# Layer 3 of a four-layer graph network makes its messages by rows of 128 edges into a ring

## The chip, the cores and the metric

The kernel runs on one core of one Trainium2 chip. The metric is device time in microseconds (us) of one execution. The engines are TensorE (PE, with its weight loads as PEld), VectorE (DVE), ScalarE (ACT), GpSimd (POOL) and SyncE (SP, which here only issues DMAs and waits).

## The reference

Four residual layers on 6250 nodes with 128 features and 100,000 edges, sorted by their target node. Each layer normalizes, applies relu, passes messages along the edges and adds the result. Layer 3 is the one that changes:

```python
s = s @ (w_lin1_s / sqrt(32));  v = einsum('nui,uw->nwi', v, w_lin1_v / sqrt(32))   # per node
h = silu(edge_scalars @ (fc_w1 / sqrt(8))) * SILU_NORM       # 8 -> 64, per edge
w0, w1, w2, w3 = split(h @ (fc_w2 / sqrt(64)), 4)            # 64 -> 4 x 32
se, ve = s[edge_src], v[edge_src];  es, ev = edge_attr[:, :1], edge_attr[:, 1:4]
mid_s0 = w0 * se * es;              mid_s1 = w3 * einsum('eui,ei->eu', ve, ev) / SQRT3
mid_v0 = (w1 * se)[:, :, None] * ev[:, None, :];   mid_v1 = (w2 * es)[:, :, None] * ve
ns, nv = segment_sum(mid_scal, edge_dst) / 4, segment_sum(mid_vec, edge_dst) / 4
x = x + concat(ns @ w_lin2_s, nv @ w_lin2_v)
```

A message has 256 numbers per edge.

## The kernel before, in words

The edges stand in DRAM as 782 rows of 128. Nodes are in 50 blocks of 128. As edges are sorted by target, a row belongs to one block or to a few that follow each other. The setup makes a list of items, one for each pair of a row and a block that it touches: 832 places in all (`ITEMS`), 208 groups of four (`QUADS`). A row that touches two blocks stands in two items. Tables per item lie in SBUF: source nodes `src_it`, target within the block `rel_it`, and as registers' food the block (`blk_row`) and the row (`row_row`).

Layer 3's edge loop works by quads of items. In step q, in the order of each engine's own list:

- SP (`load_small_rows`, lines 449 to 465) waits for DVE and ACT to be done with quad q-8 (two calls of `held`, each a wait and a semaphore increment, lines 240 to 243) and loads for each of the four items its row of `e_a8` (L463) and of `e_a4` (L464). Every fourth quad it loads 16 registers with row numbers (L455).
- POOL (L670) gathers table rows by source node into `G`, a ring of 16 items, four DMAs per quad; it waits for the products of the quad four before.
- PE: first layer of the MLP of quad q-1 (L871), transpose of the attributes of quad q (L878), aggregation of quad q-4 by a one-hot matrix (L887), second layer of the MLP of quad q-2 (L897).
- ACT: copies the transpose (L1075), applies silu (L1080), scales messages (L1087, L1091).
- DVE (`edges3`, lines 1517 to 1574): adds the four aggregates of quad q-5 to the accumulator of their blocks (helper at L1388), with a register load of block numbers every fourth quad (L1524), products of quad q-3 (L1545, L1551, L1563, L1567, L1569, L1572), one-hot of quad q-1 (L1375).

The messages lie in `msg3`, a ring of four quads, and are read at the place where they were written. `quad_steps` (L268) writes the loop: 8 steps ahead, a hardware loop of 8 steps per turn, the rest behind. No planner is at work; the order is the written one, and each engine waits on semaphores that count the others' steps. Before the loop, SP loads the MLP's weights (`load_fc`, L467) and stores the node tables (`store_table`, L370). After it, `node_updates` multiplies by `w_lin2` and adds to `X`, 13 batches of up to four blocks, and SP stores each.

Layers 1 and 2 have loops of the same kind, and gather at L670 too.

Of the kernel before, what the change touches and what calls it, by code (L numbers as in the profile page):

```python
# [25 lines left out]
P = 128  # L26
N = 6250
E = 100000
D = 128
# [22 lines left out]
QUADS = ITEMS // 4  # L52
NODE_BATCH = (4, 4, 2, 4)
# [4 lines left out]
def gnn_layers(nc, x, src, dst, edge_attr_4, edge_attr_64, edge_attr_8, edge_weight,  # L58
               W0, gamma, beta, Wmsg, bmsg, Wupd, bupd, w1, b1, w2, b2, wg, bg, wu, bu,
               wl1s, wl1v, fc1, fc2, wl2s, wl2v, out):  # L60
    with ExitStack() as ctx:
# [8 lines left out]
        def dram(name, shape, dt=F32):  # L70
# [4 lines left out]
        e_a4, e_a8, e_a64 = dram("e_a4", [2 * EPAD, 4]), dram("e_a8", [2 * EPAD, 8]), dram("e_a64", [2 * EPAD, 64])  # L75
        e_pre = dram("e_pre", [QUADS + 4, P, 4, 256])
# [6 lines left out]
        X = sb("X", [P, NBT, D])  # L83
        big = sb("big", [P, BIGW])
# [4 lines left out]
               big[:, 0:NBT * L3W].rearrange("p (b f) -> p b f", f=L3W)]  # L89
# [51 lines left out]
        spare3 = big[:, NBT * L3W:BIGW]  # L141
        fc1q = spare3[0:32, 0:256].rearrange("p (a b) -> p a b", b=P)
        fc2q = spare3[:, 256:512]
        pr3 = spare3[:, 512:2560].rearrange("p (s j c t f) -> p s j c t f", s=2, j=4, c=2, t=4)
        msg3 = spare3[:, 2560:6656].rearrange("p (s j f) -> p s j f", s=4, j=4)
        tmp3 = spare3[:, 6656:6912].rearrange("p (j t f) -> p j t f", j=4, t=2)
        sum3 = spare3[:, 6912:7040].rearrange("p (j f) -> p j f", j=4)
# [44 lines left out]
        inputs_in, weights_in, const_ready, x_in = sem("inputs_in"), sem("weights_in"), sem("const_ready"), sem("x_in")  # L192
# [90 lines left out]

        def landed(each, ring, q, k, lag):
# [62 lines left out]
        def _(sp):  # L347
# [5 lines left out]
            sp.wait_ge(x_in, 1)  # L353
# [95 lines left out]
            def load_small_rows():  # L449

                ph = EDGE[3]
                regs = [sp.alloc_register(f"arow_{k}") for k in range(RING)]

                def top(item):
                    sp.load(regs, row_row[0:1, bass.ds(item + LEAD, RING)])  # L455

                def body(q, k, live):
                    if live(8):
# [1237 lines left out]
```

## Time and profile before

| what | value |
|---|---|
| median of 3 runs (lowest, highest) | 6580.35 us (6579.94, 6586.99) |
| profiled execution, own time | 6581.73 us |
| its span (first to last instruction) | 6580.1 us |
| mean granted TensorE clock | 0.718 of 2.4 GHz |
| busy: PE, DVE, ACT, POOL | 4451.8, 3511.6, 1918.0, 3778.7 us |
| gathers at L670 (three layers) | 2496, 2417.5 us busy, mean 969 ns |

How to read the rows further down. A row of busy time by stretch has the window, its length, then the busy us (and count) of PE, PEld, DVE, ACT and POOL, the granted clock of PE, the mean busy share of the DMA engines and GB/s. A row of waits has the total us, how often, and the longest. A row of a group has count, busy us and mean ns, then the engine's idle time before it and what ended most of it. A row in order of time has start, duration, engine, line and operation; "SPq" is SP's queue, and a bracket tells the idle time before. In the chain, "issue" is time in which the engine waited for nothing that the profile shows.

### The profile page before, as it was taken

Reading aid. Unit: us, or ns where it says so; the run is one execution under the profiler, and the core shown is the slowest. Engines: PE = TensorE matmul, PEld = TensorE weight load, DVE = VectorE, ACT = ScalarE, POOL = GpSimd, SP = SyncE. Lnnn points to the kernel's source line nnn. Section 1 sums busy time; section 2 is a strip of 40 time slices with the busy share of each in tenths; the row PEclk is TensorE's granted clock in tenths of the full one; section 3 lists DMA queues with packets and bytes.
Section 4 is the critical chain, followed back from the end, with each engine's and each line's share of the span. In section 5 each row is a group of like instructions: output and inputs, shape, how many; then the busy total and the mean of one; then the engine's idle time right before and its main releaser. Section 6 shows DMA issues by size and latency. Waiting matters only on the chain. (4 is left out here: it accounts for less than half of the span.)

```text
span 6580.1 us, 113728 instructions
## 1 busy us (share of the span) xinstructions
PE 4451.8 (68%) x21582; PEld 3403.9 (52%) x21583; DVE 3511.6 (53%) x11197; ACT 1918.0 (29%) x5540; POOL 3778.7 (57%) x3395
## 2 busy tenths in 40 slices
PE   1888888888345555656777777777765666666667
PEld 1666666666234444444565656565554444444445
DVE  5655555555443232332655655555565555656555
ACT  2322222222122222222322222222243333333333
POOL 2888888888356666665255555555515454555443
PEclk9555555555577777777889888888886667777667
DMA  4666665666434454444244444444412222222222
GB/s 135 101 90 93 89 93 92 90 92 90 95 112 152 155 156 152 154 154 148 97 138 139 140 136 138 136 141 134 137 55 39 37 38 37 37 38 37 37 38 44
DMA packets 822279, 660.17 MB, mean 100 GB/s; under 512 B 444329, under 2 KB 711251, under 8 KB 820826
## 3 DMA queue, kind: packets, MB, share of 16 engines
q0 software_dynamic: 214432, 287.62, 22.0%
q1 hardware_dynamic: 607674, 370.53, 20.3%
q10 hardware_dynamic: 96, 1.20, 0.1%
q8 instruction: 24, 0.39, 0.0%
q14 instruction: 53, 0.43, 0.0%
HBM read 464.78 MB, written 225.68 MB: 105 GB/s over the span
## 5 line engine op out<-in xcount | busy, mean ns | idle before, releaser
L670 POOL DMA_INDIRECT G<-table,src_it x2496 | 2417.5, 969 | 2121.0 <-issue 651.1
L1388 DVE TENSOR_TENSOR big<-psum,big 128x129 f32 (+2 forms) x2496 | 823.6, 330 | 1225.0 <-remote 596.0
L642 POOL DMA_INDIRECT sums<-work,idx x832 | 1284.1, 1543 | 318.4 <-issue 179.2
L800 PE MATMUL psum<-work 128*128 128x128 f32 x1664 | 631.0, 482 | 192.8 <-DVE work L1435 115.0
L887 PE MATMUL psum<-big,oh 128*128 128x256 f32 x1664 | 643.7, 554 | 8.2 <-ACT big L1091 3.5
L1037 ACT ACTIVATE work<-psum,work 128x128 f32<-128x128 f32 x832 | 305.4, 367 | 1066.4 <-PE psum L792 667.4
L800 PEld LDWEIGHTS psum<-work 128*128 128x128 f32 x1664 | 414.0, 308 | 384.0 <-DVE work L1435 243.5
L747 PE MATMUL psum<-We,work 64*128 64x256 f32 x1664 | 347.0, 552 | 375.1 <-ACT work L1016 295.0
L1375 DVE TENSOR_TENSOR oh<-iota,rel_it 128x512 f32<-128x512 f32 x625 | 438.5, 702 | 298.5 <-remote 143.5
L792 PE MATMUL psum<-big,work 128*128 x1664 | 586.1, 455 | 0.0
L887 PEld LDWEIGHTS psum<-big,oh 128*128 128x128 f32 x1664 | 444.7, 280 | 134.0 <-issue 41.8
L1427 DVE TENSOR_SCALAR work<-G,src_it 128x128 f32<-128x128 int32 x832 | 268.3, 322 | 392.1 <-PE psum L800 308.6
L878 PE MATMUL psum<-ident,work 128*32 128x128 f32 x208 | 69.0, 332 | 557.3 <-DMA work<-e_a 431.6
L747 PEld LDWEIGHTS psum<-We,work 64*128 64x128 f32 x1664 | 212.9, 268 | 435.8 <-issue 352.5
L792 PEld LDWEIGHTS psum<-big,work 128*128 128x128 f32 x1664 | 414.2, 309 | 26.3 <-issue 8.7
L784 PE MATMUL psum<-ident,oh 128*128 128x128 f32 x832 | 366.3, 440 | 83.8 <-issue 46.9
L1050 ACT ACTIVATE work<-psum 128x512 f32<-128x512 f32 x208 | 124.2, 597 | 969.4 <-remote 512.2
L820 PE MATMUL psum<-big,work 128*128 x2496 | 377.0, 300 | 31.2 <-ACT work L1063 28.0
L1009 ACT ACTIVATE work<-psum 128x256 f32<-128x256 f32 x208 | 79.7, 383 | 970.0 <-remote 480.6
L1075 ACT ACTIVATE work<-psum 32x128 f32<-32x128 f32 x208 | 55.4, 266 | 1019.5 <-PE psum L878 676.4
L1493 DVE TENSOR_TENSOR work<-psum,work 128x512 f32<-128x512 f32 x416 | 267.2, 684 | 157.8 <-remote 72.9
L1435 DVE COPY work<-psum 128x128 f32<-128x128 f32 x832 | 242.5, 291 | 179.8 <-DMA sums<-work,idx 172.5
(230 smaller groups left out, 7709.9 us busy)
## 6 DMA issues: line engine op xcount, KB each, us to landing
e_pre<-work SPq DMA_DIRECT2D x208, 512.0 KB
work<-e_pre SPq DMA_DIRECT2D x208, 512.0 KB
G<-e_src SPq DMA_DIRECT2D x832, 64.0 KB
G<-table,src_it POOLq DMA_INDIRECT x2496
work<-e_a SPq DMA_DIRECT2D x832, 32.0 KB
e_a<-in_edge_attr_dram SPq DMA_DIRECT2D x51, 488.0 KB
sums<-work,idx POOLq DMA_INDIRECT x832
work<-e_a SPq DMA_DIRECT2D x832, 4.0 KB
```

Of the source, the lines that this page charges most:

```text
L642: pool.indirect_dma_start(sums[k % COPIES], bass.IndirectOffsetOnAxis(ap=idx[:, k:k + 1], axis=0), z_out[:, k, :], None, compute_op=ALU.ad ...
L670: pool.indirect_dma_start(G[:, k, 0:wid], None, tab, bass.IndirectOffsetOnAxis(ap=src_it[:, n:n + 1], axis=0)).then_inc(quad_in[k // 4], 16)
L747: mm = t.matmul(bank[5 + j % 2][:, j // 2 * 256:j // 2 * 256 + 256], eT1[h:h + 64, (k - 1) % 2, j // 2, :], We2[h:h + 64, :], start=True, ...
L784: t.transpose(bank[s % 2][:, 0:P], oh[:, s, :], ident[:]).then_inc(ph["t_done"], 1)
L792: t.matmul(bank[2 + s % 2][:, 0:P], ohT[:, s % 4, :], at(Tz, b), start=True, stop=True).then_inc(ph["row_done"], 1)
L800: t.matmul(bank[4 + s % 2][:, 0:P], same[:, s % 4, :], scaled[:, s % 4, :], start=True, stop=True).then_inc(ph["sum_done"], 1)
L820: mm = t.matmul(bank[1 + j // 2][:, j % 2 * 256:j % 2 * 256 + 256], ohT2[:, j, :], Qp[:, bass.ds(b, 1), piece * 256:(piece + 1) * 256].rea ...
L887: mm = t.matmul(bank[4 + k % 2 * 2 + j // 2][:, j % 2 * 256:j % 2 * 256 + 256], oh[:, k % 4 * 4 + j, :], msg3[:, k % 4, j, :], start=True, ...
L1037: a.activation(scaled[:, s % 4, :], bank[2 + s % 2][:, 0:P], ACT.Copy, scale=w_it[:, bass.ds(n - 4, 1)]).then_inc(ph["w_done"], 1)
L1375: v.tensor_tensor(oh[:, k % 4 * 4:k % 4 * 4 + 4, :], iota[:].unsqueeze(1).broadcast_to([P, 4, P]), rel_it[:, bass.ds(q * 4, 4)].unsqueeze( ...
L1388: v.tensor_tensor(to, ps, to, ALU.add).then_inc(EDGE[layer]["acc_done"], 1)
L1427: v.tensor_scalar(same[:, s % 4, :], src_b[:, s, :], src_it[:, bass.ds(n - 1, 1)], None, ALU.is_equal).then_inc(ph["same_ready"], 1)
```

## The change

Layer 3 separates what depends only on an edge from what depends on an item. Gather, MLP and products go by rows in their own order: 782 rows, 196 quads (`ROWS4`; the last holds 2). Their messages go to a ring of 64 rows (`RING3`). One-hot, aggregation and adds still go by 832 items; PE reads, for each item, its row from `row_row` and takes the ring's slot row % 64.

- SP loads four rows of an attribute with one DMA, two DMAs per quad, without registers of row numbers.
- POOL gathers with `src_row`, source nodes by row, 782 times. The setup makes this table: two more DMAs on POOL, seven more transposes and copies. It waits in DRAM (`row_cols`) until layer 3.
- PE loads 16 registers every fourth quad (`top`) and reads `msg3` at a slot worked out from them.
- The ring takes 16,384 floats per partition. So `X` and `big` become one tensor, the accumulator of layer 3 moves to the end, and blocks 22 to 49 of `X` (`KEEP` = 22) go to DRAM (`x_keep`) before layer 3's tables are stored and come back after the loop. `pr3`, `tmp3`, `sum3` and the MLP's weights move into `work`.
- `row_steps` writes 16 steps ahead, a hardware loop of 16 steps per turn, and the rest; it tells steps that are live for rows from steps live for items.

```diff
+ROWS4 = (ROWS + 3) // 4
+LAST4 = ROWS - 4 * (ROWS4 - 1)
+RING3 = 64
+KEEP = (NBT * (D + L3W) - RING3 * L3W) // D
...
-        X = sb("X", [P, NBT, D])
-        big = sb("big", [P, BIGW])
+        x_and_big = sb("x_and_big", [P, NBT * D + BIGW])
+        X = x_and_big[:, 0:NBT * D].rearrange("p (b f) -> p b f", f=D)
+        big = x_and_big[:, NBT * D:NBT * D + BIGW]
...
-        msg3 = spare3[:, 2560:6656].rearrange("p (s j f) -> p s j f", s=4, j=4)
+        msg3 = x_and_big[:, KEEP * D:NBT * (D + L3W)].rearrange("p (r f) -> p r f", f=L3W)
+        src_row = view(6144, [META]).bitcast(I32)
...
+        def row_steps(eng, depth, top, body):
+            for q in range(16):
+                if q % 4 == 0:
+                    top(4 * q)
+                body(q, q, lambda lag: q >= lag, lambda lag: q >= lag)
+            whole = ROWS4 // 16 * 16
+            with eng.Fori(16, whole, 16) as q:
+                for k in range(16):
+                    if k % 4 == 0:
+                        top(q * 4 + 4 * k)
+                    body(q + k, k, lambda lag: True, lambda lag: True)
+            for q in range(whole, depth):
+                if q % 4 == 0:
+                    top(4 * q)
+                body(q, q % 16, lambda lag: q - lag < ROWS4, lambda lag: q - lag < QUADS)
...
             def load_small_rows():
-                    for j in range(4):
-                        r = sp.snap(regs[k % 4 * 4 + j], min_val=0, max_val=ROWS - 1)
-                        sp.dma_start(a8q[:, k, j, :], e_a8[bass.ds(r * P, P), :]).then_inc(attr3[k], 16)
-                        sp.dma_start(a4q[:, k, j, :], e_a4[bass.ds(r * P, P), :]).then_inc(attr3[k], 16)
-                quad_steps(sp, 0, top, body, 8)
+                    n = LAST4 if isinstance(q, int) and q == ROWS4 - 1 else 4
+                    at_rows = slice(q * 4 * P, q * 4 * P + n * P) if isinstance(q, int) else bass.ds(q * (4 * P), 4 * P)
+                    for to, of in ((a8q, e_a8), (a4q, e_a4)):
+                        sp.dma_start(to[:, k % 8, 0:n, :], of[at_rows, :].rearrange("(j p) f -> p j f", p=P)).then_inc(attr3[k % 8], 16)
+                row_steps(sp, ROWS4, lambda item: None, body)
...
                 if layer == 3:
                     load_fc()
+                    sp.dma_start(x_keep, X[:, KEEP:NBT, :]).then_inc(kept, 16)
+                    sp.dma_start(src_row, row_cols).then_inc(kept, 16)
+                    sp.wait_ge(kept, 48)
                 if layer:
                     store_table(layer)
                 else:
+                    sp.dma_start(row_cols, m_row).then_inc(kept, 16)
+                    sp.wait_ge(kept, 16)
...
                 barrier(sp)
                 if layer == 3:
+                    sp.dma_start(X[:, KEEP:NBT, :], x_keep).then_inc(kept, 16)
...
-                for n in range(ITEMS):
+                for n in range(ROWS if layer == 3 else ITEMS):
...
+                    of = src_row if layer == 3 else src_it
...
             def edges3():                                     # PE
+                regs = [pe.alloc_register(f"mrow_{k}") for k in range(RING)]
+                def top(item):
+                    pe.load(regs, row_row[0:1, bass.ds(item + (LEAD - 16), RING)])
...
                         for j in range(4):
+                            slot = pe.snap(regs[k % 4 * 4 + j], min_val=0, max_val=ROWS - 1) % RING3
                             mm = t.matmul(bank[...], oh[:, k % 4 * 4 + j, :],
-                                          msg3[:, k % 4, j, :], start=True, stop=True)
+                                          at(msg3, slot), start=True, stop=True)
...
+                row_steps(pe, QUADS + 4, top, body)           # ACT: ROWS4 + 3, DVE: QUADS + 5
...
                     else:                                     # DVE, node_updates of layer 3
                         dve.wait_ge(ph["mm_done"], i + 1)
+                        if b + n > KEEP:
+                            dve.wait_ge(kept, 64)
```

## Rows read from the trace of the kernel before

**Rows 1.** Busy by stretch: edge loops 1, 2, 3, then the end

```profile
1870.00:3110.00 1240.00, 723.54 (x3706) 556.60 (x3706) 369.28 (x1026) 280.51 (x618) 788.97 (x827) 0.73 0.49 152
3300.00:4825.00 1525.00, 1118.43 (x7429) 913.69 (x7430) 912.53 (x1811) 446.01 (x804) 776.89 (x784) 0.89 0.45 136
4930.00:6541.00 1611.00, 1026.05 (x4369) 727.12 (x4369) 943.17 (x2494) 557.68 (x2081) 795.46 (x831) 0.70 0.21 37
6541.00:6580.00 39.00, 35.03 (x300) 34.84 (x300) 8.67 (x13) 13.69 (x26) 0.00 (x0) 0.94 0.29 83
```

**Rows 2.** Who waited for whom, 5200 to 6400 us

```profile
ACT work L1075 <- PE psum L878: 505.0, 117, 9.7
```

**Rows 3.** Chain of waits in the edge loop of layer 3

```profile
by line: issue 36.4%; SPq L464 24.8%; SPq L463 19.2%; SPq L462 5.6%; SPq L242 3.4%; SPq L243 3.3%; SPq L455 2.6%; SPq L274 1.1%; PE psum L887 0.7%; another core or an unknown queue 0.5%; DVE big L1388 0.4%; DMA work<-e_a 0.3%; ACT big L1091
```

**Rows 4.** Line 1545: count, ns min/median/max, first and last start

```profile
L1545 DVE TENSOR_TENSOR big<-psum,G x208: 411/423/427, 4956.1 to 6532.2; 128x256 f32<-128x256 f32 x104
```

**Rows 5.** SP and POOL in order of time, 5833 to 5846 us

```profile
5833.73 0.94 POOL L670 DMA_INDIRECT G<-table,src_it  x1 [4.98 <-DVE big L1551]
...
5835.78 0.72 SPq L464 DMA_DIRECT2D work<-e_a  x1
...
5840.14 0.72 SPq L463 DMA_DIRECT2D work<-e_a  x1
5841.62 0.71 SPq L464 DMA_DIRECT2D work<-e_a  x1
...
5842.92 0.94 POOL L670 DMA_INDIRECT G<-table,src_it  x1 [0.31 <-issue]
...
5845.38 0.33 SPq L463 DMA_DIRECT2D work<-e_a  x1
5845.90 0.33 SPq L464 DMA_DIRECT2D work<-e_a  x1
```

**Rows 6.** Groups of instructions, 5200 to 6400 us

```profile
L670 POOL DMA_INDIRECT G<-table,src_it x626 | 599.8, 958 | 600.5 <-DVE big L1551 445.6 <-issue 155.0
L1388 DVE TENSOR_TENSOR big<-psum,big 128x256 f32 x624 | 259.1, 415 | 274.0 <-remote 134.5 <-issue 69.9 <-PE psum L887 69.6
L1375 DVE TENSOR_TENSOR oh<-iota,rel_it 128x512 f32<-128x512 f32 x156 | 113.6, 728 | 0.0
```

**Rows 7.** DVE in order of time, one step with nothing missing

```profile
5808.03 0.42 DVE L1545 TENSOR_TENSOR big<-psum,G 128x256 f32<-128x256 f32 x1 [2.35 <-issue]
...
5812.65 0.41 DVE L1545 TENSOR_TENSOR big<-psum,G 128x256 f32<-128x256 f32 x1
```

**Rows 8.** The register load on DVE in this loop

```profile
L1524 DVEq TENSOR_LOAD <-blk_row x53: 1097/1102/1110, 4960.8 to 6537.4; - x53
```

**Rows 9.** Busy in two short stretches, then PE in the second

```profile
5802.30:5808.10 5.80, 3.54 (x21) 2.57 (x21) 3.32 (x10) 2.65 (x10) 3.77 (x4) 1.00 0.23 38
5815.70:5819.40 3.70, 3.70 (x9) 2.53 (x8) 1.05 (x4) 2.65 (x10) 2.79 (x4) 0.50 0.19 48
5815.71 3.78 PE L887 MATMUL psum<-big,oh 128*128 128x256 f32 x8
5819.42 1.23 PE L897 MATMUL psum<-big,work 64*128 64x128 f32 x8
```

**Rows 10.** Two DMAs with more pieces: ns min/median/max

```profile
L375 SPq DMA_DIRECT2D table<-work x51: 359/360/410, 1838.5 to 4926.6; - x51
L354 SPq DMA_DIRECT2D X<-in_x_dram x1: 895/895/895, 4.3 to 4.3; - x1
```

**Rows 11.** GB/s in 40 slices of 1712 to 1800 us

```profile
GB/s 0 199 310 290 291 290 290 290 290 290 290 290 291 290 290 290 290 290 290 290 290 226 0 0 0 0 0 0 0 7 0 0 0 0 0 0 0 0 0 0
```

**Rows 12.** SP ahead of the tables of layer 3

```profile
4888.06 1.22 SPq L473 DMA_DIRECT2D big<-in_L_gnn_fc_w_dram  x2
...
4907.43 0.41 SPq L375 DMA_DIRECT2D table<-work  x1
```

**Rows 13.** Copies of one of three item tables in the setup

```profile
110.50 1.57 DVE L1285 CAST src_it<-psum 128x128 int32<-128x128 f32 x7 [0.60 <-PE psum L695]
```

More of the change, by code:

```diff
@@ L451, in load_small_rows, with body @@
                 ph = EDGE[3]
[L452 to L458, printed above, removed]
+                def body(q, k, row, item):
+                    if row(8):
                         held(sp, ph["vec_done"], 3 * q - 21)
                         held(sp, ph["es_done"], 2 * q - 14)
-                    for j in range(4):
-                        r = sp.snap(regs[k % 4 * 4 + j], min_val=0, max_val=ROWS - 1)
-                        sp.dma_start(a8q[:, k, j, :], e_a8[bass.ds(r * P, P), :]).then_inc(attr3[k], 16)
-                        sp.dma_start(a4q[:, k, j, :], e_a4[bass.ds(r * P, P), :]).then_inc(attr3[k], 16)
-                quad_steps(sp, 0, top, body, 8)
+                    n = LAST4 if isinstance(q, int) and q == ROWS4 - 1 else 4
[3 more added lines that the diff above has]
+                row_steps(sp, ROWS4, lambda item: None, body)
             def load_fc():
@@ L660, in _ @@
                 if layer == 3:
-                    g.memset(spare3[:, 0:512], 0.0).then_inc(fc_zero, 1)
-                g.memset(big[:, 0:NBT * wid], 0.0)
+                    g.memset(fc_both, 0.0).then_inc(fc_zero, 1)
+                g.memset(flat3(acc[layer]), 0.0)
                 barrier(pool)
@@ L687, in _ @@
             mm.then_inc(meta_T, 1)
-            m_f = big[:, 3 * META:6 * META]
+            m_f = big[:, 3 * META:7 * META]
             pe.wait_ge(meta_rel, 1)
-            for q in range(3 * CHUNKS):
+            for q in range(4 * CHUNKS):
                 b = q % 6
@@ L862, in edges3, with body @@
                 pe.wait_ge(fc_ready, 1)
-                def body(q, k, live):
-                    if live(1):
-                        if live(2):
+                regs = [pe.alloc_register(f"mrow_{k}") for k in range(RING)]
+                def top(item):
+                    pe.load(regs, row_row[0:1, bass.ds(item + (LEAD - 16), RING)])
+                def body(q, k, row, item):
+                    if row(1):
+                        if row(2):
                             pe.wait_ge(ph["hid_done"], q - 1)
@@ L899, in body @@
                         mm.then_inc(ph["w_done"], 1)
-                quad_steps(pe, 4, lambda item: None, body, 8)
+                row_steps(pe, QUADS + 4, top, body)
                 barrier(pe)
@@ L1090, in body @@
                         for j in range(4):
-                            last = a.activation(msg3[:, o % 4, j, 0:P], pr3[:, o % 2, j, 0, :, :].rearrange("p t f -> p (t f)"),
+                            last = a.activation(msg3[:, o % 16 * 4 + j, 0:P], pr3[:, o % 2, j, 0, :, :].rearrange("p t f -> p (t f)"),
                                                 ACT.Copy, scale=a4q[:, o % 8, j, 0:1])
                         last.then_inc(ph["es_done"], 1)
-                quad_steps(act, 3, lambda item: None, body, 8)
+                row_steps(act, ROWS4 + 3, lambda item: None, body)
                 barrier(act)
@@ L1524, in top, with body @@
                     dve.load(regs, blk_row[0:1, bass.ds(item + (LEAD - 20), RING)])
-                def body(q, k, live):
+                def body(q, k, row, item):
                     def add(j):
                         add_item(3, regs[k % 4 * 4 + j], bank[4 + (k - 1) % 2 * 2 + j // 2][:, j % 2 * 256:j % 2 * 256 + 256],
-                                 4 * q - 20 + j if live(6) or j else None)
+                                 4 * q - 20 + j if item(6) or j else None)
                     o = k - 3
@@ L1572, in body @@
                         v.tensor_tensor(to[:, :, 1, :], to[:, :, 1, :], sum3, ALU.add).then_inc(ph["vec_done"], 1)
[L1573 removed]
+                row_steps(dve, QUADS + 5, top, body)
                 barrier(dve)
```

118 lines of the change are left out of this document (65 added, 53 removed).

## The prediction

> **What bounds the kernel now.** I read four views. The busy time by stretch comes first [rows 1]: the edge loop of layer 3 runs from 4930 to 6541 us, a quarter of the span, and in it no engine is full. DVE is busy 943 of 1611 us, POOL 795, PE 1026 with a granted clock of 0.70, the DMA engines 21%. Such a loop is held by something that doesn't count as busy. The waits say by what [rows 2]: the longest is ACT's copy L1075, which waits for PE's transpose L878, and that transpose takes in the rows of `e_a8` that SP loads. The chain of waits names their issuer [rows 3]: SP's own instructions (L464, L463, L462, L243, L242, L455) are 60% of it and most of the 36% "issue" is the time between them. So the loop goes at the pace at which SP issues eight small DMAs per quad (four items). The first L1545 starts at 4956.1, the last at 6532.2, 208 in all [rows 4]: 7.61 us per quad.
>
> SP has two speeds [rows 5]. POOL gathers without a pause from 5833.73 to 5843.86. In that burst SP's DMAs start at 5835.78, 5840.14 and 5841.62, and only two more come before 5845.38: 1.5 us apart, some 1.9 on average over those last ones, and 4.4 where the four wait instructions of `held` lie between. After the gathers have stopped the next two are 0.52 us apart. That decides much below, for the change both relieves SP and lets POOL gather with fewer pauses.
>
> **What paces it once SP doesn't.** Four limits per quad.
> - POOL: the eight gathers of that burst start 9.19 us apart from first to last, with one of 1.40 us among them [rows 5]; the mean one is 0.96 us, and 155 us of "issue" over 500 of them are 0.31 more [rows 6]: 4 x 1.27 = 5.07 us.
> - DVE: where nothing is missing, L1545 starts at 5808.03 and again at 5812.65 [rows 7], 4.62 us, and every fourth quad has a register load of 1.10 us [rows 8]: 4.9 us.
> - PE: a whole quad at 2.4 GHz (granted 1.0) is the 3.54 us busy of the first row of [rows 9]. At 1.2 GHz (granted 0.5) aggregation L887 takes 3.78 us and the product L897 1.23; with the small ones, which I put at 1.6, that is 6.6.
> - SP, below.
>
> **The change, part by part.**
> 1. *SP's loads.* Two DMAs per quad of rows in place of eight, no register load, no row arithmetic; per quad SP keeps two `held` (four instructions) and two DMAs of three instructions: 10 against about 28. At the fast pace that is 2 x 0.52 + 0.3 = 1.4 us instead of 4.5. At the slow pace it is one step of 4.36 us and one of 1.5 to 2.1 [rows 5]: 5.8 to 6.5 us. A DMA now covers 512 pieces; the table store L375 does as well and takes 0.36 us to issue, and L354 with 49 blocks 0.90 [rows 10], so I price the larger shape at nothing (bound 0 to 0.5 us each). The number of pieces stays, and with all DMA engines at 21% [rows 1] they are hidden.
> 2. *Fewer products.* 196 quads of rows, not 208, run gather, MLP and products. One-hot, aggregation and adds still run for 208 quads, so 14 steps at the end (199 to 212) hold only those. Such a step is about 4 x 0.42 + 0.73 on DVE [rows 6] plus a quarter of a load, 2.7 us (2.3 if they overlap in part), and at most L887 at 1.2 GHz plus the load, 4.1 [rows 8, 9]; I take 3.0, nearer the DVE row: 42 us.
> 3. *PE reads the ring by register.* It adds one register load per four quads (priced like DVE's, 1.10 us [rows 8], 0.28 per quad) and the arithmetic of a slot per item. That can run ahead of the array: I take 0, and as the far end one more load per quad, 1.1. PE at 2.4 GHz comes to 3.8 us (4.9), below POOL; at 1.2 GHz to 6.9.
> 4. *Start of the loop.* The first product is at 4956.1 [rows 4], some 26 us in, because body 3 needs 32 DMAs issued during the first burst of gathers. After, 8. It can't be below 10 (four gathers of 1.27, then three steps) nor above 26; I take 18.
> 5. *Rest of the features.* 28 of 50 blocks, 1.83 MB, and `row_cols`, 0.46 MB, move before the tables of layer 3. Big loads ran at 290 GB/s [rows 11]: 8 us, issued behind `load_fc` at 4889.3 [rows 12], so landed by about 4900. SP now waits for them, and its table stores and the barrier are queued behind. The first store starts at 4907.43 [rows 12]. Cost 0; at a third of the rate 5 us. On the way back 1.83 MB take 6.3 us from the barrier, and the first batch that needs them is the sixth of 13 in 39 us [rows 1], some 15 us in or later: 0.
> 6. *Setup.* POOL issues two more DMAs behind its indirect loads (priced like gathers, 2.5 us), seven more transposes pass PE and DVE (1.57 for seven copies), and DVE casts 896 more columns (less than that again) [rows 13]. With their landing 3 to 10 us, I take 6. `row_cols` goes out beside the tables of layer 0.
>
> **The sum.** How often is PE at 1.2 GHz? Layer 2's loop, where PE is 73% busy (as 3.8 of 5.07 us would be), shows a granted clock of 0.89 [rows 1], which is 22% of the time at the lower level. Then a quad takes 1 / (0.78/5.07 + 0.22/6.9) = 5.4 us if SP never holds. If gathers ran without pause SP would hold at 5.8 to 6.5, mid 6.15. Truth is between, as any pause of POOL of a microsecond or two lets SP load several quads ahead (its ring holds eight). Layer 1's loop is the nearest row: 208 quads in some 1240 us, 6.0 us each, with POOL busy 64% beside its 0.31 gaps, and with 5 DMAs of SP per quad [rows 1]. I take the middle of 5.4 and 6.15: 5.8 us. Loop: 18 + 195 x 5.8 + 42 + 1 = 1192 us against 1611, minus 419. With setup plus 6, minus 413. The profiled execution took 6581.7 us (span 6580.1): 6169. The median of the runs is 1.4 us lower: I say 6167.
>
> The Trainium skill speaks against the main term. "DMA: Bandwidth & Descriptors", section "Issuing engines are not separate DMA queues", says the sequencer's time to initiate a DMA is usually small relative to the DMA itself. By it the transfers pace the loop, and merging them brings nothing. Here the trace doesn't agree: the DMA engines are 21% busy and SP's issue is the chain [rows 1, 3]. It is a rival all the same. The same page, "Latency and other measured facts", gives a register load a floor near 0.6 us; by that PE's new load would be 0.15 us a quad rather than 0.28, and neither shows while POOL needs 5.07.
>
> **Rivals.**
> - *POOL paces it cleanly.* SP gets far enough ahead and the clock stays up: 5.07 to 5.45 us per quad, 195 x 0.73 to 0.35 less than forecast: 6025 to 6100. For it: DVE and PE fit under 5.07. Against: no loop of this kernel with gathers comes near it; layer 1's is at 6.0, layer 2's at 7.3.
> - *SP or a slow PE paces it.* Steady gathers keep SP at 0.7 us per instruction, or pauses around the two register loads keep PE at 1.2 GHz (6.9 us): 6.15 to 6.9 us, 6235 to 6380.
> - *Transfers pace it*, the rule above: packets pass as before, so a quad stays at 7.6, and only rows for items count: 18 + 195 x 7.6 + 43 = 1543, and 6581.7 - 68 + 6 = 6520.
> - *Issue time grows with the pieces of a DMA* (the other side). If four times the pieces took four times 0.33 us, each DMA adds 1.0; on SP's slow 6.15 that gives about 8.2 us per quad: 18 + 1599 + 43 + 6 = 1666, 55 over: 6635. It turns slower above 7.9 us per quad ((1611 - 6 - 61)/195). Against it: rows 10.
>
> **How the numbers follow.** Forecast (5.45 to 6.15 us, 6100 to 6235): 0.52. POOL: 0.17. SP or PE: 0.22. Transfers: 0.03. Issue by pieces: 0.04. The last 0.02 is for something that eats it all. 0.2%, some 13 us, is what can be told from no change. Faster 0.94, same 0.02, slower 0.04. Range: low end inside the POOL case, 6050; high end inside the SP/PE case, 6310.
>
> **What would show it.** In the trace after: SP's instructions gone from the chain, POOL's gathers (L670's successor) or PE in it; gathers 782, spaced 1.25 us in long bursts; L1545's starts 5.4 to 6.2 us apart, 196 of them; 14 quick steps at the end; granted clock of the loop 0.8 to 0.9. Wrong if the transposes still wait for the attribute DMA with SP at 0.7 us per instruction, if the clock is below 0.7, or if stretches outside the loop move by more than 15 us.

## The result and the profile after

| | before | after |
|---|---|---|
| median (lowest, highest), 4 runs each | 6583.0 us (6579.9, 6587.0) | 6388.1 us (6381.1, 6398.3) |
| ratio, 95% interval | | 0.9706 (0.9692 to 0.9721) |
| span of the profiled execution | 6580.1 us | 6379.4 us |
| loop of layer 3, first gather to last add | 4928.6 to 6540.4: 1611.8 us | 4949.5 to 6340.7: 1391.2 us |
| first product to last, per quad | 1576.1 / 207 = 7.61 us | 1339.2 / 195 = 6.87 us |

The change is 195 us faster, where 413 were forecast, and 6388 lies above the range. The spans differ by 200.7 us: the loop gives 220.6, layer 3 starts 20.9 later, and what follows the loop takes 1.0 less.

Busy time by stretch after, as in [rows 1] (edge loops 1, 2, 3), then the steps that hold items only, then the end:

```profile
1880.00:3122.00 1242.00, 701.39 (x3722) 539.49 (x3718) 369.19 (x1029) 281.72 (x621) 787.80 (x827) 0.75 0.49 153
3310.00:4850.00 1540.00, 1120.53 (x7427) 911.86 (x7425) 912.17 (x1815) 445.06 (x803) 783.74 (x784) 0.88 0.45 135
4949.00:6341.00 1392.00, 977.01 (x4212) 705.70 (x4212) 913.89 (x2413) 539.38 (x1961) 759.84 (x782) 0.74 0.22 41
6299.00:6341.00 42.00, 29.20 (x112) 20.86 (x111) 32.48 (x77) 2.23 (x8) 0.00 (x0) 0.96 0.00 1
6341.00:6379.00 38.00, 33.73 (x300) 33.31 (x300) 8.76 (x14) 13.57 (x26) 0.00 (x0) 1.00 0.43 134
```

In the loop again no engine is full: DVE 914, POOL 760 and PE 977 of 1392 us. The product L1545 is L1591 now, and this answers [rows 4]:

```profile
L1591 DVE TENSOR_TENSOR work<-psum,G x196: 412/424/426, 4959.4 to 6298.7; 128x256 f32<-128x256 f32 x196
its engine sat idle before it (us, times) until:
  remote: 308.6, 84
```

Who waited for whom, 5000 to 6200 us (total, times, longest), and then the chain by line in the loop, cut off by the view itself; they answer [rows 2, 3]:

```profile
ACT work L1119 <- remote: 437.6, 87, 5.3
POOL G L709 <- DVE work L1597: 333.6, 88, 4.3
PE psum L941 <- DVE work L1597: 293.8, 87, 4.8
DVE work L1591 <- remote: 271.7, 76, 4.5
```

```profile
by line: another core or an unknown queue 24.1%; issue 23.5%; DVE work L1597 9.1%; DVE x_and_big L1434 8.6%; DVE work L1609 4.7%; DVE x_and_big L1613 4.6%; DVEq L1570 4.0%; PE psum L931 2.4%; DVE oh L1421 2.3%; DVE work L1615 2.3%; ACT x_an
```

SP is out of the chain, as it should be. In its place stands a releaser that the profile can't name: "remote" or "another core or an unknown queue". There is one core, so the name means only that the increment which ended the wait came long after the instruction that makes it had ended. The two waits are 87 and 76 in 175 quads, every second quad. One of them in order of time (start, length, instruction, idle before it):

```profile
5498.60 0.94 POOL L709 DMA_INDIRECT G<-table,work  x1 [3.81 <-DVE work L1597]
...
5499.66 0.28 PE L921 MATMUL psum<-ident,work 128*32 128x128 f32 x1
...
5500.58 0.25 ACT L1119 ACTIVATE work<-psum 32x128 f32<-32x128 f32 x1
...
5505.04 1.23 PE L941 MATMUL psum<-work 64*128 64x128 f32 x8
...
5507.34 0.39 PE L921 MATMUL psum<-ident,work 128*32 128x128 f32 x1
...
5507.81 0.94 POOL L709 DMA_INDIRECT G<-table,work  x1 [0.30 <-issue]
5510.33 0.27 ACT L1119 ACTIVATE work<-psum 32x128 f32<-32x128 f32 x1 [4.72 <-remote]
5510.34 0.42 DVE L1591 TENSOR_TENSOR work<-psum,G 128x256 f32<-128x256 f32 x1 [4.10 <-remote]
...
5512.29 0.94 POOL L709 DMA_INDIRECT G<-table,work  x1 [3.54 <-DVE work L1597]
```

POOL gathers two quads without a pause, 5498.60 to 5508.75. PE's product L941 is over at 5506.27, and its transpose L921 at 5507.73. DVE, which needs the first, and ACT, which needs the second, both go on at 5510.33, 1.6 us after the last gather has ended. The trace also records when a semaphore is incremented. From those events, 5000 to 6200 us, the time from the start of the matmul that signals to its increment:

| products L941 and L914, by time since the burst's first gather | count | a tenth below, median, a tenth above, us |
|---|---|---|
| 0 to 2 us | 173 | 0.30, 0.43, 0.44 |
| 6 to 7 us | 30 | 4.7, 4.9, 5.2 |
| 7 to 8.5 us | 140 | 3.5, 4.3, 4.5 |

So PE computes in time, but these increments reach nobody until the burst is over; they come 1.4 to 1.9 us after its last gather. I call them held.

Some increments have no record (L931 has 132 for 208), so here is the same by who goes on. In this stretch there are 86 bursts of eight, and in all 86 the product L941 that ends 5 us or more into the burst lets DVE's L1591 start only 1.5 to 2.3 us after the last gather. Signals early in a burst are not held: behind each of the 50 transposes that end 2.0 to 2.5 us in, ACT's L1119 starts 0.04 us later. Between 2.5 and 5 us PE signals next to nothing, so when the hold begins is not shown. A few increments of the aggregation L931, which ends at 6 to 7 us, are recorded inside a burst.

The period follows: eight gathers 10.15 us, 1.6 to the release, product and its two multiplies 1.95 until POOL may go on, 13.7 us per two quads, 6.87 per quad.

### The profile page after: what moved, and what is told of

The parts are those of the page before. It is cut to its first block and busy times, and to the rows that moved or that the text cites. A ratio compares the mean times of both kernels' runs of the same rounds, so it can differ in the third digit from the quotient of the medians.

```text
span 6379.4 us, 109603 instructions
## 1 busy us (share of the span) xinstructions
PE 4373.1 (69%) x21433; PEld 3353.3 (53%) x21434; DVE 3484.0 (55%) x11121; ACT 1899.2 (30%) x5420; POOL 3753.8 (59%) x3348
## 5 line engine op out<-in xcount | busy, mean ns | idle before, releaser
L709 POOL DMA_INDIRECT G<-table,src_it x1664 | 1626.9, 978 | 1311.2 <-DVE work L1526 525.4
L1434 DVE TENSOR_TENSOR x_and_big<-psum,x_and_big 128x129 f32 (+2 forms) x2496 | 827.1, 331 | 992.0 <-remote 386.1
L709 POOL DMA_INDIRECT G<-table,work x782 | 759.8, 972 | 606.2 <-DVE work L1597 365.4
L931 PE MATMUL psum<-x_and_big,oh 128*128 x1664 | 586.3, 514 | 75.2 <-ACT x_and_big L1135 35.8
L831 PE MATMUL psum<-x_and_big,work 128*128 x1664 | 585.7, 454 | 0.0
L931 PEld LDWEIGHTS psum<-x_and_big,oh 128*128 128x128 f32 x1664 | 414.5, 262 | 181.5 <-issue 108.3
L831 PEld LDWEIGHTS psum<-x_and_big,work 128*128 128x128 f32 x1664 | 411.7, 307 | 33.8 <-issue 9.3
L941 PE MATMUL psum<-work 64*128 64x128 f32 x1568 | 190.3, 378 | 327.1 <-DVE work L1597 326.9
L859 PE MATMUL psum<-x_and_big,work 128*128 x2496 | 370.8, 296 | 42.0 <-ACT work L1107 24.7
L941 PEld LDWEIGHTS psum<-work 64*128 64x128 f32 x1568 | 143.5, 255 | 425.3 <-DVE work L1597 368.1
```

Source lines behind the costliest of these rows:

```text
L709: pool.indirect_dma_start(G[:, k, 0:wid], None, tab, bass.IndirectOffsetOnAxis(ap=of[:, n:n + 1], axis=0)).then_inc(quad_in[k // 4], 16)
L831: t.matmul(bank[2 + s % 2][:, 0:P], ohT[:, s % 4, :], at(Tz, b), start=True, stop=True).then_inc(ph["row_done"], 1)
L859: mm = t.matmul(bank[1 + j // 2][:, j % 2 * 256:j % 2 * 256 + 256], ohT2[:, j, :], Qp[:, bass.ds(b, 1), piece * 256:(piece + 1) * 256].rea ...
L931: mm = t.matmul(bank[4 + k % 2 * 2 + j // 2][:, j % 2 * 256:j % 2 * 256 + 256], oh[:, k % 4 * 4 + j, :], at(msg3, slot), start=True, stop= ...
L941: mm = t.matmul(w3[:, j, :, :].rearrange("p c f -> p (c f)"), hid3[h:h + 64, k % 2, j % 2 * P:j % 2 * P + P], fc2q[h:h + 64, 2 * h:2 * h + ...
L1434: v.tensor_tensor(to, ps, to, ALU.add).then_inc(EDGE[layer]["acc_done"], 1)
```

## The experiments

There are eighteen runs in five sessions, each session on one chip with the kernel before beside the others. Sessions differ far more than kernels, and only kernels of one session are compared. T is the time per quad of layer 3 from the profile, first product to last.

| session, kernel before | kernel | median us | ratio to before (95%) | T us |
|---|---|---|---|---|
| 1: 5423.0 | e1_ring8 | 5405.2 | 0.9968 (0.9956 to 0.9979) | 5.14 |
| | e2_pause | 5800.3 | 1.0697 (1.0679 to 1.0714) | 7.14 |
| | e3_spload | 5464.4 | 1.0075 (1.0055 to 1.0095) | 5.42 |
| | e6_spaced | 5502.2 | 1.0145 (1.0125 to 1.0165) | 5.63 |
| 2: 6584.8 | a1_after | 6388.7 | 0.9700 (0.9678 to 0.9722) | 6.87 |
| | e1b_ring8 | 6403.9 | 0.9722 (0.9706 to 0.9738) | 6.95 |
| | e4_noattr | 6379.0 | 0.9684 (0.9668 to 0.9700) | 6.83 |
| | e7_small | 6525.4 | 0.9909 (0.9892 to 0.9925) | 7.51 |
| 3: 5424.8 | e8_wwait | 5407.4 | 0.9965 (0.9951 to 0.9979) | 5.15 |
| | e3b_spload | 5468.6 | 1.0081 (1.0061 to 1.0101) | 5.45 |
| | e6b_spaced | 5499.2 | 1.0137 (1.0117 to 1.0157) | 5.62 |
| | b1_before | 5423.0 | 0.9993 (0.9983 to 1.0004) | 5.11 |
| 4: 6451.0 | a2_after | 6273.8 | 0.9725 (0.9701 to 0.9749) | 6.79 |
| | e8b_wwait | 6166.8 | 0.9554 (0.9525 to 0.9582) | 6.23 |
| | e3c_spload | 6013.0 | 0.9319 (0.9289 to 0.9349) | 5.42 |
| 5: 6445.5 | a3_after | 6272.9 | 0.9726 (0.9708 to 0.9743) | 6.80 |
| | e10_wfirst | 6296.3 | 0.9768 (0.9748 to 0.9789) | 6.96 |
| | e6c_spaced | 6208.8 | 0.9631 (0.9608 to 0.9655) | 6.46 |

In sessions 1 and 3 increments are not held; in 2, 4, 5 and at the result they are.

### Session 1: ring, pause, loads by SP, spacing

Ring of eight quads:

```diff
+                for n in range(ROWS if layer == 3 else 0):
+                    k = n % 32
+                    if k % 4 == 0 and n >= 32:
+                        pool.wait_ge(freed, n // 4 - 7)
+                    pool.indirect_dma_start(G[:, k % 16, k // 16 * P:k // 16 * P + P], None, tab,
...
```

> The ring of gathered rows holds eight quads in layer 3 (32 slots of 128 columns) in place of four; nothing else. Theory H (held signals): while POOL gathers without a pause, TensorE's semaphore increments reach nobody, from about 2.3 us after the burst's first gather until about 1.5 us after its last (in the trace after, product L941 starts up to 2 us into a burst are signalled 0.3 to 0.44 us later, those at 6 to 8 us into it 3.5 to 5.2 us later). Only two products get through per such window, whatever the ring holds: 13.7 us per two quads stay, 6.9 us per quad, total 6370 to 6400 us. Rival R (ring and latency): a quad's product starts 20.9 us after its last gather has ended, four quads fit in the ring, so 27.6 / 4 = 6.9; with eight quads POOL's own 5.07 to 5.3 us per quad takes over: 6388 - 196 x 1.7 = about 6040 to 6090 us.

Pause until the quad before has landed:

```diff
+                    if layer == 3 and k % 4 == 0 and n:
+                        pool.wait_ge(quad_in[(n // 4 - 1) % 4], QUAD_BEFORE[3] + 64 * ((n // 4 - 1) // 4 + 1))
```

> Before the first gather of each quad of layer 3 POOL also waits until the quad before has landed. Theory H: every burst is now four gathers, TensorE's held increments come out once a quad, about 1.5 us after its last gather: 3 x 1.25 + 0.94 + 1.5 + 0.1 to 0.3 = 6.3 to 6.5 us per quad in place of 6.87, total 6388 - 196 x 0.4 to 0.55 = 6280 to 6310 us. Rival R (ring and latency, or plain throughput of POOL): less issued in the same time, so no gain: 6.9 us per quad or up to 1.5 more, total 6388 to 6680 us.

Loads by SP, one per quad, in place of POOL's gathers; DVE waits for their semaphore, and what is loaded is not what the reference would gather:

```diff
+                    if row(4):
+                        held(sp, ph["prod_done"], q - 3)
+                    sp.dma_start(G[:, k % 4 * 4:k % 4 * 4 + 4, 0:P],
+                                 e_pre[bass.ds(q, 1), :, :, 0:P].rearrange("o p j f -> p (o j) f")).then_inc(sums_in[k % 4], 16)
...
-                for n in range(ROWS if layer == 3 else ITEMS):
+                for n in range(0 if layer == 3 else ITEMS):
...
```

> In layer 3 POOL gathers nothing; SP loads, with one plain DMA per quad, as many bytes in as many pieces (512 pieces of 512 B) into the same ring slots, from another array. The rows taken by source node are left out, so the output is not the reference's. Theory H: without POOL's gathers no increment is held; DVE's own 4.6 plus a quarter of a 1.1 us load paces, 4.9 to 5.2 us per quad: 6388 - 196 x 1.7 to 2.0 = 5990 to 6060 us, and TensorE's increments arrive within 0.5 us throughout. Rival T (it is the transfers into the ring, by whatever queue, that hold or delay): 6.9 us per quad stays, about 6390 us. Rival C (the low TensorE clock): TensorE at 1.2 GHz needs 6.6 to 6.9 us busy per quad by itself, about 6330 to 6390 us, with the granted clock near 0.5.

A small operation behind each gather:

```diff
+                    if layer == 3:
+                        g.memset(bn_raw[:, 0:8, :], 0.0).then_inc(fc_zero, 1)
+                        pool.wait_ge(fc_zero, n + 2)
```

> After each gather of layer 3 POOL does a small memset and waits for it, so that gathers start some 1.6 to 1.8 us apart and not 1.25. Two forms of theory H part here. H1: a short gap lets the increments out, so that POOL's pace alone is left: 4 x 1.7 = 6.8 to 7.2 us per quad, total 6380 to 6450 us, with no increment of TensorE later than about 1.5 us. H2: the hold lasts from the first landing to the last as long as gathers follow each other even at this pace: bursts of eight take 8 x 1.7 + 3.6 = 17.2 us per two quads, 8.6 us per quad, total about 6700 to 6740 us.

None of the four met its numbers, for the expectations took a chip like that of the result, and here the kernel before took 5423 us. In session 1 no increment is held: with gathers following each other for the whole loop, those of e1's product L948 come 0.30 us (median) to 0.44 us (90% of them) after the start of the matmul that signals. That e1 runs at 5.14 us per quad therefore decides nothing about its rival R; it had to be run again. It does show what paces once nothing is held: POOL, four gathers and their issue. Where e2's time goes, its waits of 4400 to 5600 us show:

```profile
POOL G L711 <- DMA G<-table,work: 398.7, 167, 3.7
```

The pause until a quad has landed is 398.7 / 167 = 2.4 us long, so T is 3 x 1.25 + 0.94 + 2.4 = 7.1. e3 came out at 5.42, above its 4.9 to 5.2: without the gathers it waits for SP's loads of the attributes and for PE (shown for e3c_spload in session 4). e6's memset and wait cost POOL 0.12 us per gather.

### Session 2: does the length of the ring matter, does SP?

> The changed kernel itself, unaltered, next to the kernel before on the chip of this call. The first four experiments ran on a chip on which the kernel before takes 5423 us and not 6583, and on which TensorE's increments arrive within 0.44 us. Theory H with the addition that a chip either holds increments during gathers or doesn't: on a holding chip (before at 6580) again 6.9 us per quad and 6370 to 6400 us; on a chip that doesn't hold, POOL paces both kernels (5.1 to 5.3 us per quad: 208 quads before, 196 and some 50 us of item steps after), so the change is worth nothing there: 5395 to 5430 us, ratio 0.995 to 1.002. Rival: ring and latency, 6.9 us per quad on any chip, so 5400 + 196 x 1.7 = about 5740 us on the fast one.

> The ring of eight quads again, next to the changed kernel on one chip. Theory H: the ring's length is worth nothing on either kind of chip: within 0.3% of a1_after (on a holding chip 6.9 us per quad stay). Rival R (ring and latency): on a chip on which a1_after runs at 6.9 us per quad, this one runs at 5.1 to 5.3, some 330 us less.

SP loads nothing after the first eight quads, and PE waits for attributes in these eight only, so that the output is not the reference's:

```diff
-                row_steps(sp, ROWS4, lambda item: None, body)
+                for q in range(8):
+                    body(q, q, lambda lag: q >= lag, lambda lag: q >= lag)
```

> In layer 3 SP loads the attributes of the first eight quads only, which all later quads use again; the rest of the attributes is left out, so the output is not the reference's. This takes SP and its small pieces out of the loop. Theory H on a holding chip: SP paces nothing after the change, 6.9 us per quad stays, within 20 us of a1_after. Rival S (SP or its thousands of small pieces, in the slow speed beside the gathers, is what is late or what holds the increments): 5.1 to 6.2 us per quad, 130 to 340 us less than a1_after. On a chip that doesn't hold: within 10 us of a1_after by either.

Eight small loads per quad again:

```diff
-                    for to, of in ((a8q, e_a8), (a4q, e_a4)):
-                        sp.dma_start(to[:, k % 8, 0:n, :], of[at_rows, :].rearrange("(j p) f -> p j f", p=P)).then_inc(attr3[k % 8], 16)
+                    for j in range(4):
+                        ...
+                        for to, of in ((a8q, e_a8), (a4q, e_a4)):
+                            sp.dma_start(to[:, k % 8, j, :], of[rows, :]).then_inc(attr3[k % 8], 16)
```

> The changed kernel with one part undone: SP loads each row's attributes with a DMA of its own again, eight per quad (still without registers of row numbers). On a holding chip SP at 0.7 us per instruction paces again as before: eight DMAs of three instructions and two waits of two, 28 instructions against the 30-odd of before, 7.0 to 7.6 us per quad, 30 to 150 us more than a1_after. On a chip that doesn't hold SP needs about 4.5 us per quad, below POOL's 5.1: within 15 us of a1_after.

Theory H, the held increments, met all four numbers. The ring of eight is worth nothing (6403.9 against 6388.7): rival R is out. The product waits as before, by the waits of e1b_ring8, 5000 to 6200 us:

```profile
POOL G L709 <- DVE work L1604: 334.6, 87, 9.1
DVE work L1598 <- remote: 274.1, 74, 4.6
```

Without SP's loads the time falls by 10 us only, so SP and its small pieces neither pace the changed kernel nor hold the increments. Put back as eight DMAs, they cost 137 us: SP is the pace again. The chain of e7_small by line, 4960 to 6490 us:

```profile
by line: SPq L492 45.0%; issue 38.3%; another core or an unknown queue 2.9%; SPq L251 2.4%; SPq L250 2.4%; DVE x_and_big L1437 1.8%; PE psum L934 1.5%; DVE work L1600 1.0%; DVE work L1612 0.6%; DVE x_and_big L1616 0.5%; DVEq L1573 0.5%; DVE
```

So of the 196 us that session 2 shows 137 are the merged loads. The other 59 are what is left by difference: rows in place of items, with their registers gone from SP, and all else in the change.

### Session 3: the same without held increments

POOL waits for a signal of PE:

```diff
                         pool.wait_ge(freed, n // 4 - 3)
+                        if layer == 3:
+                            pool.wait_ge(EDGE[3]["w_done"], n // 4 - 2)
```

> Before the first gather of a quad POOL also waits until TensorE has signalled the weights product (w_done) of the quad three before, that is the one behind the product that set the slot free. Where increments are held during gathers this makes POOL pause until they are out; where they aren't it should cost next to nothing. Theory H on a holding chip (a1_after 6389 us there): bursts of four gathers, one hold per quad that ends 1.1 to 1.8 us after the burst: 3 x 1.25 + 0.94 + 1.1 to 1.8 + 0.1 = 5.9 to 6.6 us per quad in place of 6.87, total 6330 to 6200 us. Rival (TensorE at its low clock, or the ring of four, is the next limit at once): 6.6 to 7.2 us per quad, total 6330 to 6450 us. On a chip that doesn't hold: POOL starts a quad some 1.5 us later where TensorE is behind, 5.2 to 6.0 us per quad.

> The kernel in which SP loads as many bytes in as many pieces as the gathers of layer 3, and POOL issues nothing there (rows by source node are left out, so the output is not the reference's). Theory H on a holding chip: it is POOL's gathers that hold TensorE's increments, so none is late here and the loop runs as on the other chip, 5.4 us per quad (e3_spload), total 6390 - 196 x 1.45 = about 6100 us. Rival T (any transfers into the ring hold them, or the chip is slower in general): 6.5 us per quad or more, 6310 to 6400 us, with increments late by more than 1 us.

> The kernel in which POOL does a small memset behind each gather of layer 3, 1.38 us from gather to gather in place of 1.25 (measured on the chip that doesn't hold, 5.63 us per quad). On a holding chip, H1 (a gap of 0.43 us lets the increments out): about 5.6 to 6.0 us per quad, total 6140 to 6220 us. H2 (the hold lasts as long as gathers follow each other even so): two quads in 7 x 1.38 + 0.94 + 3.6 = 14.2 us and the two memsets, 7.1 to 7.4 us per quad, total 6430 to 6500 us. I expect H2.

> The kernel before, once more, for its trace on this chip. On a holding chip: 6583 us, 7.6 us per quad in layer 3, increments of TensorE up to 10 us late. On a chip that doesn't hold: 5423 us, layer 3's loop at POOL's pace, 5.1 to 5.3 us per quad, 208 of them; layer 2's loop as long as in the changed kernel's trace on the same kind of chip within 10 us.

Nothing is held here, so e8 shows that its wait costs nothing (5407 us, 5.15 us per quad, just below the 5.2 to 6.0 expected), and e3b and e6b repeat session 1. b1_before shows what held increments do to the whole kernel. Its first product, then its busy time from the first gather to the last add:

```profile
L1545 DVE TENSOR_TENSOR big<-psum,G x208: 411/415/426, 4329.2 to 5386.1; 128x256 f32<-128x256 f32 x104
```

```profile
4310.00:5395.00 1085.00, 857.96 (x4369) 623.75 (x4370) 929.43 (x2497) 562.10 (x2081) 816.73 (x832) 0.84 0.31 55
```

5.11 us per quad, with the eight small DMAs. The same stretch of e8_wwait took 1056 us for 196 quads and the item steps. The SP of this trace has one speed; its DMAs start 0.52 us apart beside unbroken gathers, and its register operation L464 never takes long, where at the result it did (ns min/median/max; first b1_before, then the kernel before at the result):

```profile
L464 SPq FUSED_REGOPS  x832: 37/37/47, 4312.6 to 5353.0; - x167
```

```profile
L464 SPq FUSED_REGOPS  x832: 3/37/734, 4930.2 to 6516.1; - x167
```

The slow SP of [rows 5] and the held increments come and go together. In order of time, e8_wwait's ACT follows the transpose at once, with gathers on either side:

```profile
4804.59 1.13 POOL L711 DMA_INDIRECT G<-table,work  x1 [0.30 <-issue]
...
4805.99 0.39 PE L923 MATMUL psum<-ident,work 128*32 128x128 f32 x1
4806.02 0.98 POOL L711 DMA_INDIRECT G<-table,work  x1 [0.30 <-issue]
4806.42 0.27 ACT L1121 ACTIVATE work<-psum 32x128 f32<-32x128 f32 x1 [0.44 <-PE psum L923]
```

### Session 4: is it the gathers, and can POOL's pause be had?

> The changed kernel next to e8 and e3 in one session. Two kinds of session are known by the kernel before: 6583 us (increments held) and 5424 us (not held). Held: 6388 us, ratio 0.970, bursts of eight gathers, 6.87 us per quad. Not held: POOL paces it at 5.15 us per quad as it does the kernel before at 5.11, so 196 x 5.15 + 50 of item steps against 208 x 5.11, nothing to gain: 5405 to 5425 us, ratio 0.996 to 1.001.

> POOL also waits, before a quad's first gather, for the signal of the weights product three quads before. Where increments are not held it cost nothing (5407 us, 5.15 us per quad). Where they are, theory H: bursts of four, one hold per quad: 5.9 to 6.6 us per quad, 6200 to 6330 us against 6388. Rival (TensorE's low clock or the ring of four is the next limit): 6.6 to 7.2 us per quad, 6330 to 6450 us. Not held: 5400 to 5415 us again.

> SP loads the same bytes in the same pieces, POOL gathers nothing in layer 3 (rows by source node left out, so the output is not the reference's). Where increments are not held it took 5.45 us per quad in layer 3. Where they are held in the other layers, theory H (POOL's gathers hold them): 5.4 to 5.6 us per quad in layer 3, TensorE's increments there within 0.5 us, total about 6100 us. Rival T (transfers of any queue, or a session that is slower in general): 6.5 us per quad or more, increments over 1 us late, 6310 us or more.

Increments were held. The totals of a2 and e3c are 114 and 87 us below those expected and e8b's is 33 us below its range, for they were reckoned from a changed kernel at 6388 us, which takes 6273.8 in session 4. T of a2 is 6.79 where 6.87 was expected; the other two are within their ranges. e3c_spload settles the cause: without POOL's gathers layer 3 runs at 5.42 us per quad, as in sessions 1 and 3, and its 196 product signals come at most 0.45 us after the start of their matmul, although as many bytes pass in as many pieces. PE's transposes wait for SP's attribute loads there instead, 151.9 us in 98 waits between 4950 and 5850 us. In the same execution layer 2, where POOL gathers, has its increments held (3300 to 4700 us; in layer 3, 4860 to 5979 us, no wait is for "remote"):

```profile
ACT work L1098 <- remote: 417.7, 75, 8.3
```

SP's register operation beside its loads shows that SP's slow speed goes with the gathers as well (ns min/median/max in layer 3; first a2_after, then e3c_spload):

```profile
L489 SPq FUSED_REGOPS  x352: 3/17/721, 4929.6 to 6119.8; - x176
```

```profile
L493 SPq FUSED_REGOPS  x352: 37/47/56, 4939.8 to 5892.0; - x176
```

What a gather does that holds them is not shown: no run has POOL busy with something else, or with plain DMAs. Busy time of layer 3's loop, first a2_after, then e3c_spload:

```profile
4852.00:6240.00 1388.00, 991.95 (x4276) 718.38 (x4277) 914.95 (x2415) 541.76 (x1967) 760.05 (x782) 0.74 0.22 43
```

```profile
4860.00:5979.00 1119.00, 878.69 (x4276) 636.56 (x4277) 907.14 (x2415) 536.42 (x1967) 0.00 (x0) 0.82 0.27 53
```

e8b_wwait is the version that beats both kernels: 6166.8 us, 107 less than the changed kernel and 284 less than before. T is 6.23 as theory H had it, but not quite in its way. In order of time:

```profile
5208.79 0.94 POOL L711 DMA_INDIRECT G<-table,work  x1 [1.99 <-remote]
...
5215.18 1.40 POOL L711 DMA_INDIRECT G<-table,work  x1 [0.30 <-issue]
5216.88 0.94 POOL L711 DMA_INDIRECT G<-table,work  x1 [0.30 <-issue]
5218.13 0.94 POOL L711 DMA_INDIRECT G<-table,work  x1 [0.30 <-issue]
5220.96 0.41 DVE L1593 TENSOR_TENSOR work<-psum,G 128x256 f32<-128x256 f32 x1
5221.16 0.94 POOL L711 DMA_INDIRECT G<-table,work  x1 [2.09 <-remote]
```

Bursts of eight are still there (77 between 4900 and 6050 us), but POOL starts when the signal comes, no longer when the product behind it has freed a slot: the pause is 2.0 us and not 3.5, so 12.4 us per two quads.

### Session 5: how small a gap, and PE's order

> The changed kernel again, as the measure for the two others. Increments held: ratio to the kernel before 0.970 to 0.973, 6.8 to 6.9 us per quad of layer 3. Not held: 5400 to 5425 us, ratio 0.996 to 1.001, 5.15 us per quad.

The weights product ahead of the aggregation on PE, on top of e8 (`if item(4)` and its block move behind `if row(2)` and its block):

```diff
+                    if row(2):      # weights product of quad q-2
+                        ...
                     if item(4):     # aggregation of quad q-4
                         ...
-                    if row(2):      # weights product of quad q-2
-                        ...
```

> The kernel with POOL's wait for w_done, and in addition TensorE computes the weights product of a step (w) ahead of the step's aggregation and not behind it. Where increments are held: e8b_wwait ran at 6.24 us per quad, ratio to the changed kernel 0.983. Theory H with TensorE's order: w stands 3.8 us of aggregation (at the low clock) earlier, so more of its increments leave before the hold begins: 5.7 to 6.1 us per quad, ratio to the changed kernel 0.964 to 0.978. Rival (aggregation moves into the path instead, or TensorE at the low clock is the limit): 6.2 to 6.7 us per quad, ratio 0.98 to 1.00. Where nothing is held: POOL's 5.15 us per quad, within 0.3% of the changed kernel.

> A small memset behind each gather of layer 3, 1.38 us from gather to gather. Where nothing is held it took 5.62 us per quad, 100 us more than the ring of eight. Where increments are held: H1 (the gap of 0.43 us lets them out) 5.6 to 6.0 us per quad, 150 to 230 us less than a3_after; H2 (the hold goes on) 7.1 to 7.5 us per quad, 50 to 120 us more than a3_after. I expect H2.

e10 missed both its ranges: 6.96 us per quad is above the rival's 6.2 to 6.7 too, and it is 23 us slower than the changed kernel. The first half of theory H came true, since the product's recorded increments (174 of 196) come 0.43 us after the start of their matmul in the median and 99% of them within 1.5 us, and POOL gathers in bursts of four. The rival's first half looks right as well: aggregation, 3.78 us at the low clock, now stands right ahead of the next step's small products and DVE's adds wait for it. That this costs more than the hold gave back is argued from the waits; no run takes it apart. Its waits, 4900 to 5900 us:

```profile
POOL G L711 <- PE psum L931: 286.4, 121, 5.7
DVE x_and_big L1436 <- PE psum L943: 186.8, 95, 2.7
```

e6c missed both forms. It is 64 us faster than the changed kernel although POOL does more: 6.46 us per quad lies between H1 and H2. With gaps of 0.43 us in place of 0.31 some increments come out within a burst and others don't: of the 176 recorded ones of the product L944 (20 have no record) half come within 1.0 us of the start of their matmul and a tenth later than 7 us. How long a gap must be stays open; so does e2's pause where increments are held, which was not run again.

## Why the prediction was wrong

- *What bounds the kernel now.* Right in what stood in the chain: SP's issue of eight small DMAs. e7_small undoes just that part and is slower by 137 us. What was missed is why SP is slow. I took the two speeds of [rows 5] for a trait of SP; they are one face of the hold, and PE's increments are the other. The sign was in reach: [rows 6] has 134.5 us of idle time before the adds that end with "remote", and in layer 1's loop (1870 to 3110 us) the trace of before has more:

```profile
ACT work L1009 <- remote: 480.6, 59, 18.2
DVE big L1388 <- remote: 425.0, 103, 12.9
```

- *The failing step is the sum's "I take the middle of 5.4 and 6.15: 5.8 us".* T is 6.87: 195 x (6.87 - 5.8) = 208 us, nearly the miss of 221. The four limits were each a busy engine or SP. The fifth, a pause that POOL must make because it waits for DVE, DVE for PE's increment, and the increment for POOL's pause, was in none of them. The upper end of that middle, 6.15, took SP as the pace, and e4_noattr shows that SP's loads are worth 10 us in all in the changed kernel. The nearest row that backed the sum, layer 1's 6.0 us per quad, is a held loop itself: the same loop takes 1063.1 us in e8_wwait, 5.1 per quad.
- *POOL's 5.07.* A good size: where nothing is held POOL paces at 5.14 to 5.15 us. DVE's 4.9 was the pace in no run, so it stays untested. The part of the time at the low clock, which made 5.07 into 5.4, is not seen where POOL paces: 5.15 at a granted clock of 0.84. That pace was the rival "POOL paces it cleanly", and its mechanism holds in sessions 1 and 3, where by the same T the kernel before has 5.11 and there is next to nothing to gain.
- *Item steps at the end.* 42 us forecast; last product 6298.7 to last add 6340.7 is 42.0.
- *Start of the loop.* 18 us taken, 10 measured (4949.5 to 4959.4), the low bound.
- *PE's register load and slots.* Priced at 0: in e1 and e8 the loop runs at POOL's pace with both in it. No run takes them out alone.
- *SP's larger DMAs, the parked features, setup.* SP is not in the chain. Setup: layer 1's first gather at 1862.8 before and 1872.8 after, but 1871.2 in b1_before, so 0 to 10 us, not told apart from the scatter. Layer 2's loop went from 1570.0 to 1589.5 us between its first and last gather at the result; in session 3 it is 1147.5 in b1_before and 1145.2 in e8_wwait, its code the same. In other sessions with held increments it is 1501 to 1601. The 19.5 us stay open; I put them to no part of the change.
- *Rivals.* "SP or a slow PE paces it" had T right (6.15 to 6.9) for the wrong reason: neither is in the chain, and e4_noattr takes SP out for 10 us. "Transfers pace it" and "issue grows with the pieces" are out. The Trainium skill's rule behind the former ("DMA: Bandwidth & Descriptors", section "Issuing engines are not separate DMA queues": issue is usually small beside the transfer) agrees with session 3, where eight small DMAs per quad cost nothing (5.11 us per quad with them, 5.15 in e8_wwait without); it doesn't where increments are held, where merging them is worth 137 us.
- *What would show it.* SP out of the chain, yes. POOL or PE in it, no: a releaser without a name and DVE. 782 gathers 1.25 us apart, yes, in bursts of just eight. Clock of 0.8 to 0.9, no, 0.74. Nothing outside the loop over 15 us, no, 20.9.

## What to carry to other kernels

When no engine is full and the longest waits are for "remote", compare the end of the instruction that signals with the start of the one that waits. If the gap ends with another engine's burst, the burst is the suspect, and a run without it, like e3c, decides. An engine that issues DMAs in bursts may be made to wait for a signal that the others need: here such a wait cost nothing where nothing was held (e8) and took 107 us off where increments were (e8b). The forecast from busy times, 5.07 us per quad, held only in the sessions in which the waits have names.

## What the runs showed of the hardware

- While GpSimd issued gathers without a pause, in the sessions with held increments, TensorE's increments from 5 us or more after the first came only 1.4 to 1.9 us after the last, those up to 2.5 us after it came at once, and SyncE's instructions took 0.7 us each. Others' increments arrived in that time: in the burst from 5498.60 DVE's multiply that starts at 5502.71 released ACT at 5503.37, and in all 89 quads from 5000 to 6200 us in which this multiply ended inside a burst ACT went on at most 0.11 us later.
- Whether this happens changes from session to session: the kernel before took 6584.8 us in session 2 and 5424.8 in session 3, both on the chip with number 3. Nothing in the program sets it, and what does was not found. With it edge loop 1 takes 1241.3 us from first to last gather (a1_after) and 1063.1 without (e8_wwait), edge loop 2 1596.0 and 1145.2.
- So the change is worth 3% where increments are held. Where they aren't, the two nearest kernels, e1 and e8, gain 0.3%; the changed kernel itself had no run there.
- The Trainium skill, "DMA: Bandwidth & Descriptors", section "SWDGE vs HWDGE vs iDMA", says that a DMA issued from SyncE never touches the descriptor rings which GpSimd writes. e3c agrees as far as it goes: as many bytes issued by SP held nothing. That the rings are the place of the hold is not shown.
